# Causal attentions: where the score tiles are masked before the maximum, and in which order they come

## What is computed

```python
x = x + _L0_attn_ref(_layernorm(x), ...)   # windowed, 8 key heads
x = x + _L0_ffn_ref(_layernorm(x), ...)    # gated
x = x + _L1_attn_ref(_layernorm(x), ...)   # causal
x = x + _L1_ffn_ref(_layernorm(x), ...)    # splines
x = x + _L2_attn_ref(_layernorm(x), ...)   # causal, with rotation
x = x + _L2_ffn_ref(_layernorm(x), ...)    # latent experts
x = x + _L3_attn_ref(_layernorm(x), ...)   # full
x = x + _L3_ffn_ref(_layernorm(x), ...)    # experts
```

## Time and profile before

| what | before |
|---|---|
| median of 3 executions | 1833.18 us (1830.21 to 1836.35) |
| profiled execution, its time | 1827.52 us |
| its span | 1825.7 us |
| TensorE busy | 1608.8 us, 88% |
| VectorE busy | 1134.3 us, 62% |
| ScalarE busy | 867.9 us, 48% |
| GpSimd busy | 469.0 us, 26% |
| plain maxima, L1165 (all three `attention_quads` stages) | 768 instructions, 392.3 us |
| score tiles, L1420 | 768 matmuls, 233.9 us |
| masks on score tiles, L1423 and L1425 | 512 and 512 matmuls, 100.6 and 86.3 us |

### The profile page before, as it was taken

One profiled execution on the slowest core, in us unless ns is written; L12 is line 12 of the kernel. 1 busy time (PEld: TensorE's weight loads), 2 busy tenths in 40 slices (PEclk: granted clock), 3 DMA queues, 4 the chain that ended last, 5 costly groups with the idle time before them and its releaser, 6 DMA issues. The chain is left out here.

```text
span 1825.7 us, 28978 instructions
## 1 busy us (share of the span) xinstructions
PE 1608.8 (88%) x10726; PEld 963.0 (53%) x10726; DVE 1134.3 (62%) x2567; ACT 867.9 (48%) x1361; POOL 469.0 (26%) x596
## 2 busy tenths in 40 slices
PE   5899999799989999952999999689999999998776
PEld 2344444388866666541556665367764444443533
DVE  2787787333446666468577776355545788774475
ACT  1256565533325555532155555457761666665322
POOL 4222210033322330010333220036762522300000
PEclk9999999999989999965999999879999999999698
DMA  7452350200235424000643560211206435320322
GB/s 248 107 128 65 81 145 1 95 0 0 77 91 162 133 80 114 1 10 27 178 116 83 128 162 2 87 45 54 80 25 174 112 80 145 115 48 13 112 94 93
DMA packets 68962, 160.30 MB, mean 88 GB/s; under 512 B 10286, under 2 KB 15927, under 8 KB 67963
## 3 DMA queue, kind: packets, MB, share of 16 engines
q1 hardware_dynamic: 68826, 158.51, 30.6%
HBM read 109.05 MB, written 53.09 MB: 89 GB/s over the span
## 5 line engine op out<-in xcount | busy, mean ns | idle before, releaser
L1165 DVE TENSOR_REDUCE a_mx<-PS 128x1 f32<-128x512 f32 (+3 forms) x768 | 392.3, 551 | 188.1 <-PE PS L1425 128.1
L1362 ACT ACTIVATE a_pT<-PS 128x1024 f32<-128x1024 f32 (+3 forms) x384 | 310.2, 811 | 228.1 <-PE PS L1451 159.2
L1420 PE MATMUL PS<-a_k,a_q 64*128 64x512 f32 (+3 forms) x768 | 233.9, 415 | 16.7 <-DVE a_mx L1165 13.6
L440 DVE CUSTOM_DVE_ANT_0 PS<-PS,a_dist 128x448 f32<-128x448 f32 x256 | 156.1, 643 | 51.1 <-PE PS L685 48.7
L1442 PE MATMUL PS<-a_q,a_k 64*128 64x512 f32 (+3 forms) x768 | 174.0, 437 | 7.2 <-PEq L98 2.0
L1465 PE MATMUL PS<-a_pT,a_va 128*32 128x512 f32 (+3 forms) x1536 | 164.5, 500 | 3.1 <-ACT a_raw L1315 2.9
L590 ACT ACTIVATE a_pT<-PS 128x448 f32<-128x448 f32 (+1 forms) x256 | 124.6, 541 | 84.6 <-PE PS L708 84.2
L1442 PEld LDWEIGHTS PS<-a_q,a_k 64*128 64x128 f32 x768 | 76.0, 185 | 144.9 <-issue 70.5
L1420 PEld LDWEIGHTS PS<-a_k,a_q 64*128 64x128 f32 x768 | 109.0, 187 | 69.9 <-DVE a_mx L1165 57.0
L157 PE MATMUL PS<-cst 128*128 128x512 f32 x192 | 102.9, 667 | 36.7 <-PEq L98 28.6
L2361 POOL TENSOR_TENSOR f_h_low<-f_prod,f_h_high 128x512 fp32r<-128x512 f32 x84 | 109.9, 1315 | 60.4 <-ACT f_h_high L2548 57.6
(11 more groups left out here) (362 smaller groups left out, 3436.6 us busy)
## 6 DMA issues: line engine op xcount, KB each, us to landing
spread_scratch<-a_high SPq DMA_DIRECT2D x96, 256.0 KB, 3.0
a_q<-spread_scratch SPq DMA_DIRECT2D x96, 256.0 KB, 5.5
a_k<-spread_scratch SPq DMA_DIRECT2D x96, 256.0 KB, 6.2
f_gb<-gate_rows SPq DMA_DIRECT2D x68, 256.0 KB, 5.2
spread_scratch<-a_low SPq DMA_DIRECT2D x48, 256.0 KB, 4.0
a_q<-window_scratch SPq DMA_DIRECT2D x32, 256.0 KB, 5.6
a_k<-window_scratch SPq DMA_DIRECT2D x32, 256.0 KB, 6.4
window_scratch<-a_high SPq DMA_DIRECT2D x24, 256.0 KB, 4.7
```

Of the source, the lines that this page charges most:

```text
L440: dve.tensor_tensor_reduce(PS[:, 4 + a, 0:KW], PS[:, 4 + a, 0:KW], dt_[:, off:off + KW], 1.0, 3e38, ALU.add, ALU.min, mx[:, gg % 2, qt, 2 ...
L1165: dve.tensor_reduce(mx[:, gg % 2, qt, 2 * half + a:2 * half + a + 1], PS[:, tile_bank(t), 0:kw], AX.X, ALU.max).then_inc(max_done, 1)
L1362: act.activation(pT[:, N // 2 % 2, N % 2, :, q0:S], PS[:, 2 * (N % 2):2 * (N % 2) + 2, q0:S], ACT.Exp, scale=SCALE).then_inc(exp_done, 1)
L1420: mm = pe.matmul(ps[:, 0:kw], q[b % 2][rows, pair, qt * P:(qt + 1) * P], k[b % 2][rows, pair, 0:kw], start=True, stop=not causal)
```

## The change

The two mask matmuls of a score tile are gone in the causal stages; `scores_T` keeps its own. VectorE's maximum becomes the form of the windowed attention: it adds to the tile the last kw columns of a table of 512 in the constants, zero but for the triangle of -1e30 in its last 128, takes the maximum, and writes the sum back over the tile. The order of the tiles becomes the plain one of the full attention: four tiles of 512 columns, four of 384, four of 256, four of 128, so the two of a step have the same length. The masks that remain shrink from three to two matrices, their wait on TensorE moves behind the 24 tiles ahead of the loop, and the constants grow by 256 columns.

```diff
-C_ID, C_MQ, C_MT, C_SEL, C_ONE, C_ALL1, C_COFF, C_TOFF, C_GRID, C_IOTA, C_DSUM, C_BSUM, C_COST = (
-    0, 128, 256, 384, 512, 513, 641, 649, 713, 729, 737, 746, 755)
+C_ID, C_LATER, C_SEL, C_ONE, C_ALL1, C_COFF, C_TOFF, C_GRID, C_IOTA, C_DSUM, C_BSUM, C_COST = (
+    0, 128, 640, 768, 769, 897, 905, 969, 985, 993, 1002, 1011)
...
-        half_masks = first("half_masks", [P, 3, 2, P], BF16) if causal else None
+        half_masks = first("half_masks", [P, 2, 2, P], BF16) if causal else None
...
             j = t % (2 * TB * 2)
-            if causal:
-                far = (j // 2 % 2) ^ (j % 2)
-                long = TB - 1 - j // 8
-                return t // (4 * TB), TB - 1 - long if far else long, j // 4 % 2, j % 2
             return t // (4 * TB), TB - 1 - j // 4, j // 2 % 2, j % 2
...
                 dve.wait_ge(s_done, t + 1)
-                dve.tensor_reduce(mx[:, gg % 2, qt, 2 * half + a:2 * half + a + 1], PS[:, tile_bank(t), 0:kw], AX.X,
-                                  ALU.max).then_inc(max_done, 1)
+                tile, dst = PS[:, tile_bank(t), 0:kw], mx[:, gg % 2, qt, 2 * half + a:2 * half + a + 1]
+                if causal:
+                    dve.tensor_tensor_reduce(tile, tile, cst[:, C_LATER + S - kw:C_LATER + S], 1.0, -3e38, ALU.add,
+                                             ALU.max, dst).then_inc(max_done, 1)
+                else:
+                    dve.tensor_reduce(dst, tile, AX.X, ALU.max).then_inc(max_done, 1)
...
-                mm = pe.matmul(ps[:, 0:kw], q[b % 2][rows, pair, qt * P:(qt + 1) * P], k[b % 2][rows, pair, 0:kw],
-                               start=True, stop=not causal)
-                if causal:
-                    pe.matmul(ps[:, kw - P:kw], half_masks[rows, 0, 0, :], half_masks[rows, 1, 0, :],
-                              start=False, stop=False)
-                    mm = pe.matmul(ps[:, kw - 64:kw], half_masks[rows, 0, 1, :], half_masks[rows, 1, 1, 64:P],
-                                   start=False, stop=True)
-                mm.then_inc(s_done, 1)
+                pe.matmul(ps[:, 0:kw], q[b % 2][rows, pair, qt * P:(qt + 1) * P], k[b % 2][rows, pair, 0:kw],
+                          start=True, stop=True).then_inc(s_done, 1)
...
-                        if causal:
-                            pe.wait_ge(masks_done, 1)
                         for t in range(4 * TB + 4):
...
+                    if causal:
+                        pe.wait_ge(masks_done, 1)
                     p.units_kept()
                     p.loop()
...
-    c[:, C_MQ:C_MQ + P] = np.where(r[None, :] > r[:, None], MASKED, 0.0)
-    c[:, C_MT:C_MT + P] = np.where(r[None, :] < r[:, None], MASKED, 0.0)
+    c[:, C_LATER + S - P:C_LATER + S] = np.where(r[None, :] > r[:, None], MASKED, 0.0)
```

More of the change, by code:

```diff
@@ L43 @@
 HID3 = 128
-C_ID, C_MQ, C_MT, C_SEL, C_ONE, C_ALL1, C_COFF, C_TOFF, C_GRID, C_IOTA, C_DSUM, C_BSUM, C_COST = (
-    0, 128, 256, 384, 512, 513, 641, 649, 713, 729, 737, 746, 755)
+C_ID, C_LATER, C_SEL, C_ONE, C_ALL1, C_COFF, C_TOFF, C_GRID, C_IOTA, C_DSUM, C_BSUM, C_COST = (
+    0, 128, 640, 768, 769, 897, 905, 969, 985, 993, 1002, 1011)
 C_END = C_COST + NE
 UMAX = 2 * S - P - GLOB
-SBUF_FIRST, SBUF_END = 35968, 229376
+SBUF_FIRST, SBUF_END = 36992, 229376
 class Names:
@@ L868, in attention_quads @@
         wqk_in, wv_in = spare[:, 0:KC * WC], spare[:, KC * WC:KC * (WC + D)]
-        masks_in = (m[:, :, :, :].rearrange("p a b c -> p (a b c)")[:, 0:6 * P] if hosted else
-                    spare[:, KC * (WC + D):KC * (WC + D) + 6 * P])
+        masks_in = (m[:, :, :, :].rearrange("p a b c -> p (a b c)")[:, 0:4 * P] if hosted else
+                    spare[:, KC * (WC + D):KC * (WC + D) + 4 * P])
         unit_banks = (0, 1, 6, 7) if hosted else (2, 3, 0, 1)
@@ L1447, in scores_T @@
                         pe.matmul(PS[:, 2 * half + a, q0:q0 + 64], half_masks[rows, 0, 0, :],
-                                  half_masks[rows, 2, 0, 0:64], start=False, stop=False)
+                                  half_masks[rows, 1, 0, 0:64], start=False, stop=False)
                     for a in range(2):
@@ L1451, in scores_T @@
                         mm = pe.matmul(PS[:, 2 * half + a, q0:q0 + P], half_masks[rows, 0, 1, :],
-                                       half_masks[rows, 2, 1, :], start=False, stop=True)
+                                       half_masks[rows, 1, 1, :], start=False, stop=True)
                 mm.then_inc(st_done, 1)
@@ L1929, in _ @@
                         down(NB - 1, t, n, last_banks[t])
-                        if t == 1 and n == 3:
-                            pe.wait_ge(ahead.masks_done, 1)
                         if t and n % 4 == 3:
@@ L3178, in half_masks @@
     r = np.arange(P)
[L3179 to L3182, removed]
+    full = np.stack([np.eye(P), np.where(r[None, :] < r[:, None], MASKED, 0.0)])
+    halves = full.reshape(2, 2, 64, P).transpose(2, 0, 1, 3)
+    return np.concatenate([halves, halves], 0).reshape(P, 4 * P).astype(np.float32)
 def constant_rows():
```

## The result

The changed kernel takes 1849.2 us (median; 1841.4 to 1856.8), the kernel before, beside it, 1833.6 (1826.8 to 1836.4). The ratio is 1.0088 with a 95% interval of 1.0060 to 1.0116; measured once more, in another session, it is 1.0098 (1.0064 to 1.0131), again 1849.2 us. The forecast was 1788. It was wrong in sign: 16 us lost in place of 45 won.

A forecast was written before the change was run, and what follows sets the result against it. TensorE was taken to bound both causal attentions; 15.9 + 15.6 us from three batches each, 5 from the last batches, 5 and 3 from tiles before the loops: 44 us off 1833, rounded to 1788 (1765 to 1808; ends 1755 and 1822).

The forecast's parts named there:

- TensorE sets the pace, and what leaves it is won: In both causal attentions TensorE is busy (61.1 of 62 us in the first); time leaving it is saved until VectorE limits.
- S falls from 0.64 to 0.25 us a step: A step's two score tiles on TensorE, without mask matmuls, fall to 0.25 us: 0.39 saved a step, 12.5 a batch.
- T pairs: Unmasked matmul pairs of a step's transposed scores on the two row halves: 0.32 us for 512 columns, 0.16 for 128.
- The masked form takes VectorE no longer than the plain one, and the bank comes back 0.14 us later: VectorE's reduction of a tile: 0.63 us at 512 columns, work hardly growing; the accumulator read delays the tile's return 0.14 us.
- Rival (b): VectorE's accumulator read is not covered by the next tile: 32 us back, 1820 us; chance 0.14.
- rival (c): Writing sums back into PSUM while TensorE fills the other bank costs 0.25 us more a tile: 1833 us; chance 0.05.
- The moved lengths: Tile lengths become uneven over eight steps: VectorE is crowded in steps 4 to 7, some 2 of 3.1 us go to waits.
- The hand count: Followed steps 4 to 7, from the first score tile of step 4 to the transposed scores of step 8: 6.0 us.
- The order by length serves this: Equal lengths let both halves of a score pair start and end together, serving its fall to 0.25 us.
- Groups of eight steps at 10.6 us: Eight steps without other pieces take 10.6 us, before 11.6; four groups plus other pieces give 56.2 us a batch.
- Rival (d): TensorE's gaps in steps 4 to 7 lower its granted clock; with one half at the low level, 1890 us; chance 0.06.

The follow-up runs named there:

- e5: The kernel before, mask matmuls kept, with VectorE's maximum over only the first 64 columns of each score tile: 1791.5 us, ratio 0.9757.
- e4: The changed kernel with a plain maximum, no masks on the score tiles, and the old mixed order of lengths: 1818.5 us, ratio 0.9885.
- e6: e4 with VectorE's maximum over only the first 64 columns of each score tile: 1774.7 us, ratio 0.9670.
- F: One part of the change: VectorE's plain maximum becomes the masked form with sums written back to PSUM; costs 16.6 to 18.5 us at equal clock.
- e3: The changed kernel with a plain maximum, so no masks on the score tiles, in the plain order of lengths: 1822.5 us, ratio 0.9917.
- e10: The kernel before with only VectorE's maximum exchanged for the new form, adding zeros and writing sums back to PSUM: 1848.9 us, ratio 1.0086.
- e12: The changed kernel with mask matmuls put back on the score tiles, plain order, VectorE's new form adding zeros: 1854.7 us, ratio 1.0110.
- e7: e4 with the four mask matmuls of each step's transposed scores left out too: 1820.3 us, ratio 0.9941.
- e8: The changed kernel with the masked maximum's sums written to scratch tiles in SBUF instead of back to PSUM: 1831.0 us, ratio 0.9983.

## Why the prediction was wrong, point by point

*TensorE sets the pace, and what leaves it is won.* This reading of the earlier trace rows failed. Busy 61.1 of 62 us looked like no waiting. But e5 takes work from VectorE alone and wins 42 us, so TensorE waited for VectorE all along, 62.4 - 57.8 = 4.6 us a batch. The page of the profile warns that matmul ends are modelled, and here one sees what that does: short rows that overlap their neighbours cover the gaps. The Trainium skill (Perfetto Trace Analysis, Tensor Engine Instruction (MATMUL, LD_WEIGHTS)) says the same of TensorE's end times, and the traces agree: 46.7 us of mask rows in two batches were worth 2 x 2.6 = 5.2 us (62.44 - 59.87 a batch, before and e4).

*S falls from 0.64 to 0.25 us a step.* This is the term that carried the sum, mis-sized at both ends. 0.64 was read as the price of tiles and masks. Of the nine groups of the earlier trace rows the cheapest, 0.45 us, are what a masked pair costs when it waits for nothing (e5: 0.45 and 0.51); with the short maximum hardly a pair takes more, so what the dearer ones hold beyond it, up to 0.45 us, is a wait for VectorE. And 0.25 was taken from T pairs, of which the next instruction uses the same row halves. A score pair mostly stands ahead of matmuls on all 128 rows, and costs 0.35 to 0.41 (e6); the few in e6 that a T pair follows mostly take 0.21 to 0.25, which shows that it is the follower. So the masks' share of the 0.39 us a step was really 0.07 to 0.10, and of the 12.5 us a batch 2.6. In after an S pair comes out at 0.57 us on average (18.2 us of a batch of 32 steps, each row's start to the next row of another kind); before, 0.60.

*The masked form takes VectorE no longer than the plain one, and the bank comes back 0.14 us later.* The durations were right (starts 0.62 and 0.64 us apart against 0.63 forecast). The bank comes back 0.07 to 0.09 us later rather than 0.14: from the start of a 512-column tile to the end of its read it is 0.76 to 0.78 us, where the plain reduction takes 0.69. The price was missed all the same: F costs 17.5 us at equal clock. Rival (b) had the accumulator read at 32 us, rival (c) had the write into PSUM and called it unlikely, by the earlier trace rows. Those rows show VectorE's pace, which the write doesn't change; when the bank is free for TensorE isn't in them.

*The moved lengths.* The hand count is about right where it can be followed. From the first S of step 4 to T of step 8 it gave 6.0 us; the timeline has 642.36 - 635.88 = 6.5, and the copy of the maxima does end the wait. In the whole the plain order costs 3 to 7 us, not a gain. "The order by length serves this" was right only where TensorE waits for nothing: there pairs of 512, 384, 256 and 128 columns take 0.41, 0.35, 0.29 and 0.24 us ahead of matmuls on all rows (e3), 0.32 on average, against 0.38 for the mixed ones. But the second tile of a 512 pair waits for its bank, and such a pair ahead of the values takes 1.03 us in e3 and 1.07 in after. That is more than the others save: e3 is slower than e4.

*Groups of eight steps at 10.6 us.* With S at 0.57 in place of 0.25 in 32 steps, some 10 us a batch come back; the 6.8 us between 56.2 and 63.0 are that, less the waits that the count had already put in.

*The clock.* Rival (d) had the sign right, place and size wrong: not half of the work at the low level, and not in every batch, but short stretches, mostly in the first and last batches of the loops, and as much in stages that the change doesn't touch: 10 to 14 us, where it put 100 from the forecast. Most of the 16 us lost is this. (d)'s reason for it, the gaps in steps 4 to 7 alone, is not what the runs show: the batches from 640 to 700 us have these gaps and a clock of 1.00. The forecast gave it 0.06, on the ground that one stretch with 37.6 of 50 us busy showed 0.99. The Trainium skill (TensorE: Matmul & The Clock Gate, A second HAM failure mode: psum-queue depth-cycling) had been weighed too lightly: it tells of a clock that swings where TensorE idles briefly between groups as it cycles through banks, and after shows 0.66 to 0.89 in stretches of such loops. But the waits alone don't do it: e10 and e12 have the same form and the same two banks, wait no less, and stay at 0.946 and 0.945. What is shown is that clock and mask matmuls go together, with the new form and its sums in PSUM (0.946 to 0.937 and 0.945 to 0.933) and in e7 (0.943 to 0.928). With the plain reduction the loss is at most small (e3, e4: 0.943). Why, and why e6 with still less work keeps 0.943, stays open; a test with other small matmuls in place of the masks was not made. Nor did the low level stay out of e12 altogether: one interval of its first loop takes 19.3 us where others take 15.9.

In short, the step that failed is S from 0.64 to 0.25 us, 12.5 us a batch. The masks were worth 2.3 to 2.6, and the new form (2.0) and the order (1.0) took more than that back. The range's upper end was 1822. Rivals were held apart that in fact added: small price of the masks, late bank, and clock.

## What to carry to other kernels

To learn what an instruction costs an engine with modelled ends, find the same instruction where nobody waits, or take the other engine's work away: busy time, and the gap to the next row, mix price and wait. If a bank goes round between two engines, count an instruction until it gives the bank back, accumulator read and write included, and send a product that nobody reads to SBUF. When small matmuls leave a busy TensorE, look at the granted clock before and after, and compare kernels at equal clock.

## What the runs showed of the hardware

- A bf16 mask matmul of 64 or 128 columns behind a score tile, on one of the two row halves, holds TensorE up by 0.02 to 0.025 us (e5 and e6); its row reads 0.19 or 0.23.
- Two score matmuls on the two row halves, the longer of 384 or 512 columns, take 0.35 to 0.41 us ahead of a matmul on all 128 rows, and mostly 0.21 to 0.25 ahead of the next pair on row halves (e6).
- The accumulator read behind a VectorE form takes 138 ns if its sums go to PSUM and 83 ns if they go to SBUF. The pace of the form is the same, 0.61 us at 512 columns (after and e8). The windowed attention writes them to PSUM too; moving them was not tried there.
- The mean granted clock of one program varies from execution to execution by up to 0.02, and its time by 12.4 us per 0.01. Kernels that differ by a thousand short matmuls can differ in mean clock by 0.01 (e12 0.945, the changed kernel 0.934 and 0.932 in two sessions).
